# Two graph layers with layer norm on one core: the last batch in pairs of tiles, v with its weight halves side by side, and the transposed adjacency through GpSimd's converting queue

## What is computed

```python
v = relu(x @ Wv + bv); q = relu(x @ Wq + bq); k = relu(x @ Wk + bk)
att = softmax(q @ k.T * adj - 9e15 * (1 - adj), axis=-1)
x = layernorm(x + relu((att @ v) @ Wo + bo))
h = x @ W_w.T + W_b;  e = h @ a1;  f = h @ a2
u = adj * exp(e[:, None] + f[None, :] + a_b)
x = layernorm(x + (u / u.sum(-1, keepdims=True)) @ h)
```

## Time and profile before

| | us |
|---|---|
| median of three runs | 415.2 |
| the profiled execution | 414.7 |
| its span, first to last instruction | 413.0 |
| TensorE, VectorE, ScalarE, GpSimd busy | 394.7, 344.4, 337.1, 266.3 |
| pass 5, 210.11 to 257.44 us | 47.33 |

### The profile page before, as it was taken

How to read it: one execution, slowest core, us unless ns; L and a number is a source line. 1 busy time by engine, 2 the same in 40 slices (tenths; PEclk the granted TensorE clock), 3 DMA queues, 4 the chain that set the end, 5 groups by cost and what they waited for, 6 DMA issues and landing times.

```text
span 413.0 us, 8808 instructions
## 1 busy us (share of the span) xinstructions
PE 394.7 (96%) x2836; PEld 366.1 (89%) x2836; DVE 344.4 (83%) x1000; ACT 337.1 (82%) x642; POOL 266.3 (64%) x230
## 2 busy tenths in 40 slices
PE   8999999999999999999999999999999999998680
PEld 7898988999999999999999999999999899998580
DVE  3786898889699986989789996989969998998755
ACT  4877778998699978989799878989789888984943
POOL 1563735467449693778929695696929882961862
PEclk9999999999999999999999999999999999999696
DMA  7693626166661588354790777535591757336661
GB/s 230 234 319 115 211 110 253 53 231 240 226 225 56 195 312 283 125 184 176 256 338 17 230 266 261 215 118 189 208 347 59 254 181 229 107 99 207 203 203 51
DMA packets 37868, 80.71 MB, mean 195 GB/s; under 512 B 2752, under 2 KB 19264, under 8 KB 37824
## 3 DMA queue, kind: packets, MB, share of 16 engines
...
q10 hardware_dynamic: 144, 0.14, 0.3%
...
## 4 chain that ended last, share of the span: by engine, by line
PE 82%; DVE 13%; issue 2%; ACT 1%; DMA 1%; DVEq 0%; ACTq 0%
PE pt_ps L1413 12%; PE m_ps L1461 11%; PE av_ps L1425 7%; PE s_ps L1354 7%; PE av_ps L1426 7%; PE av_ps L1427 7%; PE s_ps L1356 6%; PE s_ps L1355 6%; PE m_ps L1361 4%; PE m_ps L1354 4%; PE m_ps L1355 3%; PE m_ps L1356 3%; DVE prob L920 2%; DVE stat L962 2%; DVE prob_tl L928 2%
## 5 line engine op out<-in xcount | busy, mean ns | idle before, releaser
L928 DVE TENSOR_TENSOR prob_tl<-pt_ps,prob_th 128x512 fp32r<-128x512 f32 x128 | 85.8, 683 | 16.8 <-ACT prob_th L622 16.3
L622 ACT ACTIVATE prob_th<-pt_ps 128x512 fp32r<-128x512 f32 x128 | 74.3, 591 | 31.3 <-PE pt_ps L1413 30.8
L920 DVE CUSTOM_DVE_ANT_0 prob<-s_ps,penalty 128x1024 f32<-128x1024 f32 x64 | 78.2, 1222 | 10.2 <-PE pt_ps L1413 4.4
L614 ACT ACTIVATE prob<-prob,neg_max 128x1024 f32<-128x1024 f32 x64 | 73.5, 1148 | 4.7 <-DVE neg_max L920 4.7
L1425 PE MATMUL av_ps<-prob_th,vh 128*128 128x256 f32 x256 | 74.6, 291 | 0.0
L1413 PE MATMUL pt_ps<-rhs,prob 128*128 128x128 f32 x512 | 73.7, 273 | 0.3 <-DVE prob_tl L928 0.2
L380 POOL TENSOR_SCALAR penalty<-adj_in 128x1024 bf16<-128x1024 f32 x64 | 66.3, 1049 | 9.9 <-DMA adj_in<-in_adj_dram 8.8
L1427 PE MATMUL av_ps<-prob_th,vl 128*128 128x256 f32 x256 | 72.4, 283 | 0.0
L1426 PE MATMUL av_ps<-prob_tl,vh 128*128 128x256 f32 x256 | 72.4, 283 | 0.0
L572 ACT ACTIVATE adj_t<-adjt_in 128x1024 fp32r<-128x1024 f32 x58 | 60.9, 1052 | 7.2 <-DMA adjt_in<-in_adj_t_dram 7.1
L1413 PEld LDWEIGHTS pt_ps<-rhs,prob 128*128 128x128 f32 x512 | 59.3, 141 | 7.5 <-DVE prob_tl L928 1.2
...
## 6 DMA issues: line engine op xcount, KB each, us to landing
adj_in<-in_adj_dram SPq DMA_DIRECT2D x64, 512.0 KB, 5.2
adjt_in<-in_adj_t_dram SPq DMA_DIRECT2D x64, 512.0 KB, 4.3
...
x_in<-in_x_dram SPq DMA_DIRECT2D x8, 512.0 KB, 4.8
...
```

Of the source, the lines that this page charges most:

```text
L614: sc.activation(prob[i % 2][:, :], prob[i % 2][:, :], ACT.Exp, bias=neg_max[:, i:i + 1], scale=-1.0, accum_out=row_sum[b % 2][:, i:i + 1]) ...
L622: sc.activation(prob_th[n % 2][:, tiles(k), (i % 2) * P:(i % 2 + 1) * P], pt_ps[k][:, :].rearrange("p (c n) -> p c n", n=P), ACT.Copy).the ...
L920: v.tensor_tensor_reduce(out=prob[i % 2][:, :], in0=s_ps[:, :, :].rearrange("p a n -> p (a n)"), in1=penalty[:, n % RING, :], scale=-1.0, ...
L928: v.tensor_tensor(prob_tl[n % 2][at], pt_ps[k][:, :].rearrange("p (c n) -> p c n", n=P), prob_th[n % 2][at].bitcast(F32), ALU.subtract).th ...
```

## The change

**v.** `project_v` works on a pair of tiles, side by side like `project_out`: two matmuls of 256 and two of 128 columns instead of six of 128. A batch has four such pieces, each in a bank. `v_out` on VectorE adds the bias to the low half (`v_low`), then the high half to it, in PSUM; a new `v_relu` on ScalarE writes the relu to `vf`. `bo_full` is bo itself, the third matmul of `form_w1` is gone.

**Transposed adjacency.** For batches 0 to 6 `load_adj_t` is issued by GpSimd, straight into the rounded ring `adj_t` (the queue converts float32 to fp32r), as soon as the sums of four tiles before are done; `aggregate` waits for the load. `round_adj` and `adjt_in` are gone. For the last batch SP loads float32 tiles into the eight 4 KB slots of `raw`, which hold xt_in, qf, kf, vf and the four slots of adj_in until then, and ScalarE rounds them in place (`round_last`; `adjt_last` lies over `raw`).

**Last batch in pairs.** out, residual, statistics, norm0, transposes, h, exp, g and the sums of batch 7 are cut in four pairs of tiles. The pair's out and h are made with `product`; g is made on ScalarE and VectorE straight from the bank. The sums come in steps of four, two and two chunks (`aggregate_first`, `aggregate_third`, `aggregate_last`). HOLD is 4 in place of 6, in four places.

**Order.** All lists of head, pass and tail are written anew on each engine, and the tables of slots with them. In the diff the lists are left out.

```diff
         w1h, w1l = w1hl[:, 0, :], w1hl[:, 1, :]
-        wb_wide, bv_wide = sb("wb_wide", [P, P]), sb("bv_wide", [P, P])
-        minus_bv, bo_full, wb_row = sb("minus_bv", [P, D]), sb("bo_full", [P, D]), sb("wb_row", [P, D])
+        wb_wide, wb_row = sb("wb_wide", [P, P]), sb("wb_row", [P, D])
+        bo_full = bo_row
         beta2, beta_sum, beta = sb("beta2", [P, 2]), sb("beta_sum", [P, 1]), sb("beta", [P, 1])
         minus_half = sb("minus_half", [P, T])
 
-        adj_in = sb("adj_in", [P, RING, N])
+
+        with ExitStack() as early:
+            raw = early.enter_context(nc.sbuf_tensor("raw", [P, T, N], F32))
+        adjt_last = sb("adjt_last", [P, T, T, P], F32R)
+        xt_in, qf, kf, vf = (raw[:, j, :] for j in range(4))
+        adj_in = raw[:, RING:2 * RING, :]
         penalty = sb("penalty", [P, RING, N], BF16)
-        adjt_in = sb("adjt_in", [P, STAGING, T, P])
         adj_t = sb("adj_t", [P, RING, T, P], F32R)
...
-            def load_adj_t(b, i):
-                n = T * b + i
-                wait(sp, adjt_done, n - STAGING + 1)
-                sp.dma_start(adjt_in[:, n % STAGING, :, :], adj_t_tiles[b, i]).then_inc(adjt_arrived[n % STAGING], 16)
+            def load_adj_last(i):
+                if i >= RING:
+                    sp.wait_ge(penalty_done, T * LAST + i + 1)
+                elif i == 3:
+                    sp.wait_ge(vl_done, 2 * B)
+                else:
+                    sp.wait_ge(*lower((xtl_done, ql_done, kl_done)[i], LAST, 1))
+                sp.dma_start(raw[:, i, :], adj_t_tiles[LAST, i].rearrange("p t d -> p (t d)")).then_inc(adjt_last_arrived[i], 16)
 
...
+            def load_adj_t(b, i):
+
+                n = T * b + i
+                wait(pool, agg_full, n - RING + 1)
+                gp.dma_start(adj_t[:, n % RING, :, :], adj_t_tiles[b, i]).then_inc(adjt_arrived[n % RING], 16)
...
-            def round_adj(b, i):
-                n = T * b + i
-                if b < LAST:
-                    wait(act, agg_full, n - RING + 1)
-                elif i < 4:
-                    act.wait_ge(s_full, T * B)
-                elif i < 6:
-                    act.wait_ge(q_full, 2 * B)
-                    act.wait_ge(k_full, 2 * B)
-                    act.wait_ge(v_full, 2 * B)
-                else:
-                    act.wait_ge(agg_full, T * (LAST - 1) + i - 1)
-                act.wait_ge(adjt_arrived[n % STAGING], 16 * (n // STAGING + 1))
-                sc.activation(flat(adj_tile(b, i)), flat(adjt_in[:, n % STAGING, :, :]), ACT.Copy).then_inc(adjt_done, 1)
+            def round_last(i):
+
+                act.wait_ge(adjt_last_arrived[i], 16)
+                sc.activation(flat(adjt_last[:, i, :, :]), raw[:, i, :], ACT.Copy).then_inc(adjt_last_done, 1)
...
+            def v_relu(b, j):
+                wait(act, vl_done, 2 * (b - 1) + j // 2 + 1)
+                act.wait_ge(v_summed, TH * b + j + 1)
+                vv = bank["v", b, j][:, :].rearrange("p (t a d) -> p t a d", a=2, d=D)
+                sc.activation(vf[:, j * PAIR:(j + 1) * PAIR].rearrange("p (t d) -> p t d", d=D), vv[:, :, 0, :],
+                              ACT.Relu).then_inc(v_evac, 1)
...
+            def norm0_pair(j):
+                act.wait_ge(shift0_done, B + j)
+                for t in range(2 * j, 2 * j + 2):
+                    sc.activation(x1[:, t, :], x1[:, t, :], ACT.Identity, bias=shift0[:, t:t + 1],
+                                  scale=rstd0[:, t:t + 1]).then_inc(x1_done, 1)
...
+            def g_hi_pair(u):
+                if u == 0:
+                    act.wait_ge(agg_full, T * LAST)
+                act.wait_ge(ef_done, 2 * LAST + u + 1)
+                for c in range(2):
+                    t = 2 * u + c
+                    sc.activation(g[:, t, 0, 0:D], bank["h_last", LAST, u][:, c * E1:c * E1 + D], ACT.Copy,
+                                  scale=ef[:, t, 1:2]).then_inc(gh_done, 1)
...
-            def v_out(b, k):
-                wait(dve, vl_done, 2 * (b - 1) + k + 1)
-                dve.wait_ge(v_full, 2 * b + k + 1)
-                v.tensor_tensor(half(vf, k).rearrange("p (t d) -> p t d", d=D),
-                                bank["v", b, k][:, :].rearrange("p (t d) -> p t d", d=D),
-                                rows(minus_bv[:, :], TH), ALU.max).then_inc(v_evac, 1)
+            def v_out(b, j):
+                if b == 0 and j == 0:
+                    dve.wait_ge(wb_arrived, 16)
+                wait(dve, v_summed, TH * b + j)
+                dve.wait_ge(v_full, TH * b + j + 1)
+                vv = bank["v", b, j][:, :].rearrange("p (t a d) -> p t a d", a=2, d=D)
+                v.tensor_tensor(v_low[:, :, :], vv[:, :, 1, :], rows(bv_row, 2), ALU.add).then_inc(v_biased, 1)
+                dve.wait_ge(v_biased, TH * b + j + 1)
+                v.tensor_tensor(vv[:, :, 0, :], vv[:, :, 0, :], v_low[:, :, :], ALU.add).then_inc(v_summed, 1)
...
+            def o_out_pair(j):
+                dve.wait_ge(o_full, TH * LAST + j + 1)
+                dve.wait_ge(inv_done, TH * LAST + j + 1)
+                for c in range(2):
+                    t = 2 * j + c
+                    o = blk(bank["o", LAST, j], c)
+                    v.scalar_tensor_tensor(out=o, in0=o, scalar=inv_sum[:, t:t + 1], in1=bo_full[:, :],
+                                           op0=ALU.mult, op1=ALU.add).then_inc(o_scaled, 1)
...
+            def g_lo_pair(u):
+                dve.wait_ge(gh_done, 2 * LAST + 2 * u + 2)
+                for c in range(2):
+                    t = 2 * u + c
+                    last = v.scalar_tensor_tensor(out=g[:, t, 1, 0:D], in0=bank["h_last", LAST, u][:, c * E1:c * E1 + D],
+                                                  scalar=ef[:, t, 1:2], in1=g[:, t, 0, 0:D].bitcast(F32),
+                                                  op0=ALU.mult, op1=ALU.subtract)
+                last.then_inc(gl_last, 1)
...
-            def project_v(b, k):
-                if b == 0 and k == 0:
+            def project_v(b, j):
+                if b == 0 and j == 0:
                     pe.wait_ge(set_ok, 2)
-                pe.wait_ge(*lower(xtl_done, b, k))
-                vv = shared("v", b, k)
-                for c in range(TH):
-                    t = k * TH + c
-                    last = product(blk(vv, c), (blk(xth, t), blk(xtl, t)), (wvh, wvl))
+                pe.wait_ge(*lower(xtl_done, b, j // 2))
+                vv = shared("v", b, j)
+                for c in range(2):
+                    t = 2 * j + c
+                    last = product_side_by_side(vv[:, c * PAIR:(c + 1) * PAIR], (blk(xth, t), blk(xtl, t)), flat(w_hl[:, 2, :, :]), D)
                 last.then_inc(v_full, 1)
 
...
+            def aggregate_first(i):
+
+                pe.wait_ge(gl_den_done, B + 1)
+                pe.wait_ge(gl_last, 2)
+                pe.wait_ge(adjt_last_done, i + 1)
                 if i < 2:
                     pe.wait_ge(z_done, T * B)
                 elif i < 4:
                     pe.wait_ge(ptl_done, 2 * T * B + i - 3)
+                elif i < EARLY:
+                    pe.wait_ge(avl_done, TH * B)
                 else:
-                    pe.wait_ge(avl_done, TH * B)
-                pe.wait_ge(adjt_done, T * LAST + i + 1)
+                    shared("agg", LAST, i)
                 sums(i, range(TH))
 
+            def aggregate_more(i, u):
+
+                pe.wait_ge(gl_den_done, B + u)
+                pe.wait_ge(gl_last, u + 1)
+                return sums(i, range(2 * u, 2 * u + 2))
+
+            def aggregate_third(i):
+                aggregate_more(i, 2)
```

1062 lines of the change are left out of this document (570 added, 492 removed), and 11 rows, old and new, of tables (HEAD_SLOTS, PASS_SLOTS).

## The result

The changed kernel takes **421.64 us** (median of 4 runs, 418.63 to 423.11), the kernel before 415.17 beside it (413.85 to 415.43). The ratio is 1.0153, 95% interval 1.0086 to 1.022: 1.5% slower. The forecast was 407, range 400 to 417; the time lies outside, on the other side of no change. A second series gave 421.89 and 1.0156 (1.0119 to 1.0194).

What follows compares the result with a forecast made beforehand. TensorE's matmuls bound a pass, a chain of VectorE, ScalarE and GpSimd steps the end. Span 413.0 - 6.1 (v) - 0.2 (form_w1) + 2.0 (tighter passes) - 3.7 (tail) = 405.0, as a run time 407 us, range 400 to 417.

Steps and rivals of the forecast that it cites:

- The step that failed: In a pass, transposed adjacency tile 5 of GpSimd's queue lands at 18 us, wanted at 20: hidden, 2 us to spare.
- Rival 3: Converting transfer lands late, twice the 4.3 us: 2 to 3 us a pass, some 12 us, 419; chance 0.13.
- v side by side: TensorE's v matmuls in project_v: 0.095 us saved a tile, 0.76 a batch, 6.1 us over 64 tiles; bounds 2.3 to 8.1.
- v on VectorE: Eight operations of about 409 ns a batch replace two of 685; VectorE grows from 41.3 to 43.6 us a pass.
- rival 2: VectorE binds: its 43.6 us cannot be packed, passes stay at 47.33, only the tail is left: 411.3; chance 0.20.
- tighter passes: Charge for VectorE's and GpSimd's fuller passes: 2.0 us in all, 0.3 a pass.
- rival 1: GpSimd becomes the bound from 1.45 us an issue; at 2.0 a pass takes 50.9 us, 429 in all; chance 0.14.
- The queue and VectorE's copies: Starving of GpSimd's descriptors in a pass: a transfer waits behind var only, a few tenths, no case of its own.
- The tail: Last batch in pairs, behind the last attend: last matmul at 397.1 us for 403.4, 3.7 us saved; bounds 0.5 to 7.

Runs made afterwards that it cites:

- Loads late: Changed kernel, with SyncE issuing the loads of x and the next batch's adjacency tiles 0 and 1 some 12 us later in a pass: 412.95 us, ratio 0.9961 to before.
- ring of five: Changed kernel, with five slots instead of four for transposed adjacency tiles, GpSimd issuing the next tile at each place: 409.32 us, ratio 0.9873 to before.

## Why the prediction was wrong, point by point

**The step that failed** is the one on the transfer: "the slot of tile 5 is free when the sums of tile 1 end, 8 us in; the issue stands behind four conversions, at about 13 us, and the tile lands at 13 + 1 + 4.3 = 18; TensorE wants it at 20. So it is hidden, with 2 us to spare". The issue came at 12.7 us and the want at 19.2, nearly as placed. The landing was 7.5 to 9.1 us, not 5.3: I took the page's median over all passes and places, from a kernel whose loads of both kinds stood in one queue in one order, for a place where the change's own order on SyncE puts 1.75 MB in the 3 us in front of it and 0.5 MB right behind. The median hid a spread too. The trace of the kernel before, on all loads of these tiles:

```profile
DMA to landing us min/median/max: 3.2/4.3/8.1
```

Each piece stood in what I had read: four conversions in a row free four slots, and the rows behind them in SyncE's new order are 0.5 MB each. "Loads late" gives 5.3 to 5.7 us at the same place, near the 1 + 4.3, though by luck, since the issue is 0.6 and not 1. A sum of bytes would have warned: the two adjacency loads that went away there are 1 MB, by the 407 GB/s of the window 2.6 us, and x, which went with them, 1.3 more; the landings differ by 2.3 to 3.8.

**Rival 3** was the case that came, with the mechanism as written ("lands late", "2 to 3 us a pass", some 12 us, 419). Its 12 us came as 8.3 of waits in five passes and 3.0 by the clock's falls, which stood in it nowhere. That 419 was 2.6 us short is, to within half a us, the last batch's own waits (2.3) and v's smaller gain (1.5), less the 0.7 between 12 and 11.3. At 0.13 it had too small a chance; a margin of 2 us made from a median should not have carried 0.53.

**v side by side**: right in kind, too large. 4.6 us measured for 6.1 (bounds 2.3 to 8.1). The side-by-side blocks of "loads late" are 2.22 us for eight tiles with a wait of 0.21 for a bank in them, so 0.25 a tile where I had 0.236: the blocks were priced well. The old form, cut into four short blocks, takes 2.87 us, 0.36 a tile where I had 0.331 from two long ones. That is 0.86 a pass, of which the wait takes 0.21 back, for the 0.76 forecast. A pass gained only 0.33 over before (47.00 for 47.33). I had not priced the neighbours: the transposes of p, those of x1 and h are each 0.1 to 0.2 us longer per pass than before, out and the sums 0.1 shorter; that the new order does it is argued, not shown. The page of the Trainium skill that I cited (TensorE: Matmul & The Clock Gate, LDWEIGHTS) gave 6.8 by weight columns alone, an estimate; the 4.6 us measured are further from it than from the sum by blocks.

**v on VectorE, and rival 2**: VectorE has 42.5 to 44.8 us in a pass (43.6 forecast), the eight new operations 418 and 432 ns (409). It did not bind: TensorE is busy 46.77 of 46.99 us in a pass of the ring of five. I charged 2.0 us for tighter passes; TensorE idles 0.2 to 0.6 us in each of the four passes shown there, 1.7 in all, 0.5 of it for a transfer.

**GpSimd, and rival 1**: an issue takes 585 ns, not 1.0 us, far from the 1.45 of the rival. GpSimd is busy 39.5 us of a pass for the 43 forecast.

**The queue and VectorE's copies.** The Trainium skill's rule that descriptors of GpSimd's queue starve during VectorE's copies (SBUF - State Buffer, Who interferes with whom) was left aside as no case of its own. The runs agree: with VectorE's work untouched the landing is 5.3 us. A rule of the Trainium skill that I did not use bears on the failed step: transfers of all queues run on the same engines and interleave (DMA: Bandwidth & Descriptors, Issuing engines are not separate DMA queues). The trace agrees: of the 3.2 MB that moved while tile 5 was under way, 2.04 were of SyncE's queue and 1.17 of GpSimd's. How much a load issued just behind a tile delays it, no run here separates.

**The tail** was right. The first matmuls behind the last attend and the first sums, on TensorE's timeline, and the windows from there:

```profile
393.04 0.38 PE L1596 MATMUL m_ps<-rhs,x 128*128 128x128 f32 x2
...
399.61 0.61 PE L1636 MATMUL s_ps<-g,adjt_last 128*128 128x258 f32 x3
```

```profile
393.04:408.94 15.90, 15.48 (x134) 15.28 (x132) 10.56 (x51) 8.67 (x26) 11.84 (x11) 1.00 0.11 34
408.94:421.40 12.46, 0.19 (x2) 0.00 (x0) 6.60 (x44) 3.51 (x8) 2.81 (x4) 0.68 0.14 43
```

Sums start 6.6 us behind the last attend (6.4 forecast), the last matmul ends 15.9 behind it (15.9), the end is 28.4 behind it (28.1); the clock stays at 1.00 up to the last matmul, 0.72 of the earlier trace rows is gone. The 3.7 us were 4 behind the last attend, and 3.0 of waits ahead of it ate most: 2.3 for adj_t, 0.7 for g. In the ring of five the last batch takes 86.2 us for 89.65: 3.4 saved.

**The sum, mended.** 407 had v 6.1 and tail 3.7 in it. With v at 4.6 it is 408.5, and the ring of five, in which TensorE waits 0.5 us in all for transfers, measures 409.3. What the forecast described is that kernel, not the one that was made.
